# Three accumulators in place of four for the edge sums of a graph block with experts

## The reference

```python
xn = layernorm(x)                                   # 12500 x 256
msgs = edge_weight[:, None] * (xn @ weight_l)[dst]  # 212500 edges
agg = segment_sum(msgs, src, 12500)                 # what the accumulators hold
x = x + (agg + bias_l + xn @ weight_r + bias_r) + mix(xn)
x = x + experts(layernorm(x))                       # top 2 of 8
```

## Time and profile before

| | us |
|---|---|
| median of 3 runs | 4696.19 |
| lowest and highest | 4651.64, 4702.84 |
| the profiled execution | 4703.04 |
| its span, first to last instruction | 4701.3 |
| first scatter, last scatter (starts) | 221.6, 3312.3 |

### The profile page before, as it was taken

The page is one execution under the profiler, slowest core; times in us unless marked ns, Lnnn a source line. Parts: engine busy times, 40 slices in busy tenths (PEclk is TensorE's granted clock), DMA queues, the critical chain, the costliest instruction groups (busy, mean ns, idle before and its releaser), DMA issues. The chain is left out here.

```text
span 4701.3 us, 86671 instructions
## 1 busy us (share of the span) xinstructions
PE 3500.7 (74%) x17027; PEld 2905.8 (62%) x17028; DVE 2486.5 (53%) x11283; ACT 1685.9 (36%) x3127; POOL 3177.1 (68%) x2213
## 2 busy tenths in 40 slices
PE   0266666667676667887888888886488839999999
PEld 0255555555555556666666666665477728887888
DVE  0577777755555656666666666665266622222222
ACT  0033333344444434444444444443011114443343
POOL 0088888888888888888888888888244424444555
PEclk9888878788888888889888888887688869999999
DMA  9388888877777777777777777776877656665554
GB/s 401 119 150 150 149 149 151 144 109 115 115 115 115 115 101 101 107 106 107 106 106 107 106 107 106 106 105 84 248 243 240 216 131 144 142 144 148 172 176 151
DMA packets 603961, 670.65 MB, mean 143 GB/s; under 512 B 62751, under 2 KB 556797, under 8 KB 599281
## 3 DMA queue, kind: packets, MB, share of 16 engines
q0 software_dynamic: 275904, 286.40, 46.7%
q1 hardware_dynamic: 269232, 283.76, 20.5%
q10 hardware_dynamic: 58752, 99.69, 5.9%
HBM read 270.03 MB, written 401.47 MB: 143 GB/s over the span
## 5 line engine op out<-in xcount | busy, mean ns | idle before, releaser
L750 POOL DMA_INDIRECT agg<-msg,sidx x1664 | 2581.3, 1551 | 725.5 <-issue 400.4
L1078 PE MATMUL bank<-rows,Cmat 128*128 x3328 | 1019.4, 447 | 168.4 <-ACT msg L1271 104.1
L1271 ACT COPY msg<-bank 128x512 f32<-128x512 f32 x832 | 486.4, 585 | 1471.0 <-DMA agg<-msg,sidx 1204.5
L1078 PEld LDWEIGHTS bank<-rows,Cmat 128*128 128x128 f32 x3328 | 694.9, 223 | 347.2 <-issue 254.5
L818 DVE SCALAR_TENSOR_TENSOR sidx<-seen_sum,trash,srcf 128x4 int32<-128x4 f32 x416 | 92.7, 223 | 1021.5 <-DMA agg<-msg,sidx 1015.7
L801 DVE TENSOR_SCALAR Emat<-bank,srcf,wtf 128x128 f32<-128x128 f32 x1664 | 565.0, 399 | 0.0
L1062 PEld LDWEIGHTS bank<-Emat,pick 128*128 128x128 f32 x3328 | 519.9, 227 | 41.0 <-issue 16.6
L1062 PE MATMUL bank<-Emat,pick 128*128 128x128 f32 x3328 | 530.9, 312 | 1.7 <-DVE seen L805 1.7
L805 DVE SCALAR_TENSOR_TENSOR seen<-bank,srcf,prior 128x128 f32<-128x128 f32 x1664 | 479.8, 342 | 0.0
L1053 PE MATMUL bank<-packed,both 128*128 (+1 forms) x416 | 187.0, 450 | 373.1 <-DVE seen L805 368.8
L1984 PE MATMUL bank<-x_xf,x_w 128*128 128x256 f32 x1792 | 407.2, 380 | 1.3 <-ACT x_xf L2012 1.3
(11 more groups left out here) (249 smaller groups left out, 4492.7 us busy)
## 6 DMA issues: line engine op xcount, KB each, us to landing
x_w<-in_L_ffn_W_dram SPq DMA_DIRECT2D x112, 512.0 KB
agg<-zeros ACTq DMA_DIRECT2D x36, 1408.0 KB, 36.2
r_agg<-agg SPq DMA_DIRECT2D x196, 256.0 KB
x_zin<-expert_table SPq DMA_DIRECT2D x112, 259.0 KB
window_raw<-in_x_dram SPq DMA_DIRECT2D x208, 128.0 KB
agg<-msg,sidx POOLq DMA_INDIRECT x1664
xn_rows<-n_xn ACTq DMA_DIRECT2D x49, 256.0 KB
xn_turned<-n_xnT ACTq DMA_DIRECT2D x49, 256.0 KB
```

The lines of the kernel that those rows point to most:

```text
L750: pool.indirect_dma_start(scratch["agg"][r][:, :], bass.IndirectOffsetOnAxis(ap=sidx[:, j:j + 1], axis=0), msg[:, j % (2 * BATCH), :], Non ...
L1078: mm = nc.tensor.matmul(M[p][:, (q % 2) * D:(q % 2 + 1) * D], Cmat[:, b % 2, q, :], rows[:, bass.ds(slot, 1), :], start=True, stop=True)
L1271: nc.scalar.copy(msg[:, at:at + 2, :].rearrange("p q c -> p (q c)"), M[p][:, :]).then_inc(s_msg, 1)
```

## The change

NACC goes from 4 to 3. 27 clears stand in place of 36. The scatter of chunk j of a group goes to accumulator (phase + j) mod 3, where phase is the group's number mod 3, so the chunks go round the three in one unbroken sequence; since 16 mod 3 is 1, POOL's loop holds three groups, each with its own phase, and groups 0 to 2, 102 and 103 are written out. `s_add` stays one semaphore for each place in a batch; a scatter at place 3 now waits for place 0 of its own batch, the others for place r + 1 of the batch before, so always for the scatter three back. SP loads three accumulators a pair, and PE sums two terms.

```diff
-NACC = 4
+NACC = 3
...
-        s_add = [sem(f"e_added{r}") for r in range(NACC)]
+        s_add = [sem(f"e_added{r}") for r in range(BATCH)]
...
-            def group(g, last=False):
+            def group(g, phase, last=False):
                 for j in range(CHUNK_GROUP):
-                    b, r = j // BATCH, j % BATCH
+                    b, r, acc = j // BATCH, j % BATCH, (phase + j) % NACC
...
-                    if not (first(g) and b == 0):
-                        pool.wait_ge(s_add[r], 16 * (NB * g + b))
+                    if r == BATCH - 1:
+                        pool.wait_ge(s_add[0], 16 * (NB * g + b + 1))
+                    elif not (first(g) and b == 0):
+                        pool.wait_ge(s_add[r + 1], 16 * (NB * g + b))
                     pool.nop(nofuse=True)
-                    pool.indirect_dma_start(scratch["agg"][r][:, :],
+                    pool.indirect_dma_start(scratch["agg"][acc][:, :],
...
-            group(0)
-            with pool.Fori(1, GROUPS - 1) as g:
-                group(g)
-            group(GROUPS - 1, last=True)
-            for r in range(NACC):
-                pool.wait_ge(s_add[r], 16 * CHUNKS // NACC)
+            for g in range(NACC):
+                group(g, g)
+            with pool.Fori(1, (GROUPS - 1) // NACC) as k:
+                for phase in range(NACC):
+                    group(NACC * k + phase, phase)
+            for g in range((GROUPS - 1) // NACC * NACC, GROUPS):
+                group(g, g % NACC, last=g == GROUPS - 1)
+            for r in range(BATCH):
+                pool.wait_ge(s_add[r], 16 * CHUNKS // BATCH)
...
-                for acc in (2, 3):
+                for acc in (2,):
                     sp.dma_start(agg[acc][:, u], pair_of(scratch["agg"][acc], i)).then_inc(s_ld2[u], 16)
...
-                pe.wait_ge(s_ld2[u], 32 * visits(i, u) + 32)
+                pe.wait_ge(s_ld2[u], 16 * visits(i, u) + 16)
...
-                        for r in (0, 2, 3):
+                        for r in (0, 2):
                             mm = nc.tensor.matmul(AT[u % 2][:, a * D + c * P:a * D + (c + 1) * P],
-                                                  agg[r][:, u, c, a * P:(a + 1) * P], ident[:], start=(r == 0), stop=(r == 3))
+                                                  agg[r][:, u, c, a * P:(a + 1) * P], ident[:], start=(r == 0), stop=(r == 2))
```

More of the change, by code:

```diff
@@ L48 @@
 assert NPAD <= P * P
-assert TILES % 2 == 0 and CHUNKS % P == 0 and CHUNK_GROUP % NACC == 0
+assert TILES % 2 == 0 and CHUNKS % P == 0 and CHUNK_GROUP % NACC == 1
 CAP = 2 * P
@@ L413, in edge_phase @@
         s_msg = sem("e_message")
-        s_add = [sem(f"e_added{r}") for r in range(NACC)]
+        s_add = [sem(f"e_added{r}") for r in range(BATCH)]
         NB = CHUNK_GROUP // BATCH
-        assert NB == 4 and BATCH == NACC and CHUNK_GROUP == 2 * WINDOW
+        assert NB == 4 and BATCH == 4 and CHUNK_GROUP == 2 * WINDOW
         wq = sb("wq", [P, HALF, D])
```

## The result

The changed kernel took 4807.16 us (median of 4 runs, 4759.32 to 4825.99) beside 4691.52 for the kernel before (4 runs, 4651.64 to 4702.84): a ratio of 1.0239, 95% interval 1.0155 to 1.0324. The forecast was 4684, range 4626 to 4752. Run once more beside thirteen runs of the kernel before, on another chip, it was at 1.0345 (1.0287 to 1.0404).

What follows compares the result with a forecast made beforehand. No engine bounds the whole span: loads beside clears set the setup, POOL's scatters the edge phase, a PE and ACT ring the route stage. 4696.2 less 12 (-24 + 73 - 61) gives 4684 us, range 4626 to 4752.

Steps and rivals of the forecast that it cites:

- Part 1: Setup before the first scatter: 27 clears instead of 36 let the loads land earlier, 24 us off (15 to 33).
- Part 2: POOL's scatters in the edge phase: three in flight instead of four makes late landings stall POOL, 73 us more (30 to 125).
- The late landing: Context stage, last scatter of a group's first batch: lands after 6.27 us beside loads, 1.49 over the 4.78 allowed.
- rival (a): Edge phase: late landings cost next to nothing, since one stall moves following scatters clear of the loads; 4621 us, chance 0.20.
- rival (b): POOL's loop: code loaded anew each lap, 0.5 us at each of 204 jumps, 102 us; 4786 us in all, chance 0.13.
- Pieces of "issue" over 1 us: POOL's idle between scatters: such pieces every 16 scatters would show that code is loaded anew each lap.
- Part 3: Route stage: one term fewer in PE's sum and one load fewer a pair, 61 us off (45 to 68).
- the 1.3 us a pair: Route stage: gain taken for each of the 47 pairs behind the first two, between 0.95 and 1.44.
- the 4.33 to ACT's copy: Route stage: us from the sum's first weight load to ACT's copy, all in the PE and ACT ring of 8.5.
- The sum: Whole kernel: 4703 - 24 + 73 - 61 = 4691 for the profiled execution, 12 less; from the median, 4684 us.
- (c): Whole kernel: upper price of late scatters together with the lower gains, 4761 us, chance 0.12.
- (d): Setup: doesn't follow the clears, SP's own issue times set it, rest as forecast; 4700 us, chance 0.07.

Runs made afterwards that it cites:

- the near waits alone: Kernel before, four accumulators and loop of one group, each scatter waiting for the third before it instead of the fourth: 4807.44 us, ratio 1.0189.
- the lap of two: Kernel before, four accumulators, POOL's loop holding two groups a lap: 4742.45 us in one run; with waits three back as well, 4896.11.
- the lap of three: Kernel before, four accumulators and its own waits, POOL's loop holding three groups a lap: 4793.30 us beside 4731.85, ratio 1.0138.

## Why the prediction was wrong

**Part 1, the setup: right.** Forecast 24 off (15 to 33), measured 27.7 and 28.2. DVE's first conversion was forecast near 125 and is at 121.2:

```profile
121.20 1.03 DVE L232 CAST flt_src<-raw_src 128x1664 f32<-128x1664 int32 x1 [115.76 <-DMA raw_end<-in_dst_dram]
```

**Part 2, three scatters in flight: the mechanism right, the size 17 us low, and one thing missed.** By themselves the waits cost 90.0 for 73, inside the ends of 30 and 125. By stage, windows from the same group to the same group (first stage, context, mix), before:

```profile
222.00:936.00 714.00, 487.78 (x2219) 397.32 (x2220) 525.61 (x2416) 228.50 (x481) 594.55 (x385) 0.82 0.86 150
996.00:1742.00 746.00, 516.22 (x2464) 427.52 (x2464) 438.08 (x2046) 329.64 (x492) 623.27 (x400) 0.84 0.76 112
1772.00:3225.00 1453.00, 1192.39 (x5372) 934.21 (x5370) 890.99 (x4114) 662.68 (x1076) 1213.87 (x784) 0.86 0.75 105
```

and with the near waits alone:

```profile
222.00:965.00 743.00, 486.09 (x2197) 399.31 (x2224) 522.34 (x2417) 228.99 (x481) 596.04 (x385) 0.80 0.83 144
1026.00:1807.00 781.00, 528.21 (x2407) 437.39 (x2457) 438.58 (x2049) 332.27 (x492) 619.40 (x400) 0.81 0.73 107
1838.00:3316.00 1478.00, 1183.99 (x5298) 936.99 (x5369) 887.15 (x4113) 663.58 (x1076) 1213.62 (x785) 0.86 0.74 104
```

24 groups of the first stage cost 29 us, 1.2 a group for 0.75; 25 of the context stage 35, 1.4 for 1.5; 49 of the mix stage 25, 0.5 for 0.35. The context stage, read from rows of its own kind, was the best. The late landing is where it was forecast, early in a group of the context stage, with its idle of 1.21 and 0.77 in place of the usual 0.3, here with the near waits alone:

```profile
1131.10 1.54 POOL L752 DMA_INDIRECT agg<-msg,sidx  x1 [1.21 <-issue]
1133.41 1.54 POOL L752 DMA_INDIRECT agg<-msg,sidx  x1 [0.77 <-DMA agg<-msg,sidx]
```

The lateness comes back in each group: rival (a), that a stall moves the scatters clear of the loads, falls. In the changed kernel the 70 pieces of idle over 0.35 that are put down to landings sum to 71 us, over the 20 that the prediction set as its sign.

**The step that failed is the one that set rival (b) aside:** "each of today's 104 groups has two of these jumps, and none shows in the idle times, so POOL's queue reaches them ahead of the engine". True of the kernel before and no evidence for the changed one, for two reasons. Those jumps land in code that has been loaded, since a lap of 205 instructions (counted in the built kernel) does not fetch anew (48 packets in all), and one of 409 or 614 does. And how far the queue is ahead is not a property of POOL: it is set by the waits, and the same change cut these from four scatters back to three. I priced the waits in Part 2 and the laps in (b), each as if the other stayed as it was. Together they cost 188; apart, 90 and 54. Rival (b) had the right mechanism with the wrong place: not 204 jumps over the gathering code at 0.5 each, but the jump back at the end of a lap, with what follows it, at (3278.6 - 3189.1) / 33 = 2.7 us a lap. Its time, 4786, came nearest to the 4807. At the 208 branches of the gathering code the changed kernel's queue stood 0.4 us in the median, and over 1 us once. Pieces of "issue" over 1 us were named as what would show it. There are 55, of which 26 stand right behind a jump back, once in 48 scatters, not in 16. But the near waits alone, with nothing loaded anew, leave 33 such pieces, so the sign did not tell (b) from late landings; the length does, 3.5 for 2.2.

The rule that the prediction cited from the Trainium skill, page "Runtime: NRT & Kernel Launch", section "Instruction fetch mechanics", that a jump out of the window of fetched code stalls for a fetch, agrees with these rows: 3.1 to 3.8 us on POOL's queue at the jumps of the long laps, 0.3 at that of the short one. What decided the cost was the cover ahead of it.

The other rule of the Trainium skill, 2.0 us plus the bytes over 436 GB/s from page "DMA: Bandwidth & Descriptors", section "Anatomy of one DMA", made no scatter late and this part free; the 90 us speak against its use beside other loads.

**Part 3, the route stage: 61 forecast (45 to 68), 42 on a chip with the higher clock and 17 on one with the lower.** The mis-sized term is the 1.3 us a pair. Of the two numbers at hand, a third of the 4.33 to ACT's copy (1.44) and a third of the weight loads (0.95), the lower was right: 7.23 - 6.27 = 0.96. The 4.33 of the earlier trace rows was no price of the sum at the full clock: from the first weight load to ACT's copy it is 3.09 us in the pair above, and 2.20 with three terms. Why it was 4.33 there, with the same 2.86 of weight loads and a granted clock of 1.00 from 3570 to 3576, stays open. And that the grant falls with the work was not in the forecast. The 89.5 us that the route stage gained in the first comparison are not this gain alone: they are two clocks as well.

**The sum** was 12 us less, and the first profile has 122.6 more. The second has -28.2 in the setup, +191.0 among the scatters, -13.2 in the routing and +50.3 behind it, together +199.9; the last 50 lie in code that the change does not touch. In nine profiles of kernels with four accumulators this stretch took 911 to 962 us (mean 935), in five with three 903 to 963 (mean 944); the kinds overlap fully. Rivals (c) and (d) did not come to pass. Two figures of the prediction don't follow from its own terms: (d) gives 4684 + 24 = 4708, not 4700, and the three prices behind the upper end of Part 2 add up to about 123, not 125. Neither changes the outcome.

What stays open: why the stretch behind the routing varies by 60 us; why the lap of two shows no second stall behind its jump, as the lap of three does; how many instructions between 205 and 409 a lap may have; and what sets a chip's share of low clock.

## What to carry to other kernels

In these kernels a loop whose code is loaded anew cost what its queue's lead did not cover. So look at both at once when a change lengthens a loop body and tightens a wait in it: for the lap of two the two together cost 197 us, where the parts alone cost 18 and 90. That nothing shows today at a jump tells of today's lead only. And before a stage's gain is read off two profiles, compare the granted clock of that stage in both.

## What the runs showed of the hardware

- POOL's code: a lap of 205 instructions left 48 packets in all on the instruction queue, laps of 409 and 614 left 296 and 278, over 50 and 33 laps. At a jump back of the long laps shown the queue stood 3.1 to 3.8 us, at one of the short lap 0.3.
- Stalls of the queue were hidden in part or whole by scatters that it had issued before them: with a lap of two, 0.36 us of a reload were left a lap with two scatters of 1.85 us in hand, 2.1 with one (17.8 / 50 and 106.8 / 50).
- The same code was granted different clocks on different chips, or at different hours (the runs don't tell these apart): 0.88 in the route stage with four terms on two chips, 0.93 on a third, and 478 against 430 us. With a third of the sum's matmuls taken out the grant on the former was 0.83 to 0.86.
- The raw arrays' loads are slow while another queue's clears are open: holding back 20 of 36 clears brought DVE's first conversion of the raw arrays from 149.3 to 84.3 us.
